# Two edits to a two-layer gated cross-attention kernel: layer-norm variance spread over all partitions, and slot-attention keys loaded from padded rows

## The reference, cut to what matters

```python
x = x + tanh(g_xattn[0]) * L0_xattn(layernorm(x), ctx, masks, ...)   # 16-head cross attention, ctx is (16, 1500, 128)
x = x + tanh(g_ffn[0])   * L0_ffn(layernorm(x), ...)                 # 16 experts, top 4, and a shared one
x = x + tanh(g_xattn[1]) * L1_xattn(layernorm(x), ctx, ...)          # slot attention, 3 rounds
x = x + tanh(g_ffn[1])   * L1_ffn(layernorm(x), ...)                 # 32 experts, top 2

def layernorm(x):            # over the 128 features, no weights
    return (x - mean(x)) / sqrt(var(x) + 1e-5)

# slot attention, three rounds, per batch: 56 slots, 1500 keys
scores = (rmsnorm(slots) @ Wq.T) @ (rmsnorm(P) @ Wk.T).T / sqrt(128)
attn   = softmax(scores, axis=slots);  attn = attn / (attn.sum(axis=keys) + 1e-6)
slots  = gru_cell(attn @ (rmsnorm(P) @ Wv.T), slots, ...)
```

## Time and profile before

| | us |
|---|---|
| three runs of the kernel before | 616.84 (median), 612.61, 617.85 |
| the profiled execution | 618.72 |
| its span | 616.9 |
| granted TensorE clock, mean over the span | 0.891 of full |

### The profile page before, as it was taken

The page is one execution under the profiler, slowest core; times in us unless marked ns, Lnnn a source line. Parts: engine busy times, 40 slices in busy tenths (PEclk is TensorE's granted clock), DMA queues, the critical chain, the costliest instruction groups (busy, mean ns, idle before and its releaser), DMA issues.

```text
span 616.9 us, 17523 instructions
## 1 busy us (share of the span) xinstructions
PE 491.4 (80%) x6216; PEld 375.7 (61%) x6216; DVE 385.0 (62%) x1149; ACT 323.5 (52%) x959; POOL 220.4 (36%) x414
## 2 busy tenths in 40 slices
PE   3687888887687899699999997889999856039990
PEld 2522224554474454289999996789899734039990
DVE  1569964555635544458989996779899845103332
ACT  3363664344322122378988986678988731023330
POOL 5366852122420000135445453435445400622241
PEclk9797987889986799989999998999999975559996
DMA  8887743343219999800000399910000099130003
GB/s 250 175 201 173 222 150 102 100 112 110 76 28 256 228 205 171 315 3 2 4 3 0 86 247 225 212 37 2 3 0 1 2 387 428 40 95 12 28 29 102
DMA packets 52589, 74.36 MB, mean 121 GB/s; under 512 B 6853, under 2 KB 46198, under 8 KB 51510
## 3 DMA queue, kind: packets, MB, share of 16 engines
q1 hardware_dynamic: 48380, 61.78, 40.9%
q0 software_dynamic: 1424, 7.81, 3.5%
q10 hardware_dynamic: 2730, 4.03, 2.2%
HBM read 69.07 MB, written 4.54 MB: 119 GB/s over the span
## 4 chain that ended last, share of the span: by engine, by line
PE 55%; DVE 13%; DMA 11%; SPq 7%; ACT 4%; issue 4%; POOL 3%; POOLq 1%; ACTq 0%; DVEq 0%
PE ps L1597 12%; PE ps L1611 8%; PE ps L1583 7%; SPq L562 6%; PE ps L1528 4%; PE ps L1727 4%; PE ps L1741 3%; DMA region<-in_wo 3%; DMA work<-in_kv_blk 3%; PE ps L1562 2%; POOL xe_scratch L746 2%; PE ps L1465 2%; DVE sumsq L991 2%; DMA region<-in_ctxT 2%; PE ps L1436 2%
## 5 line engine op out<-in xcount | busy, mean ns | idle before, releaser
L859 ACT ACTIVATE work<-ps,nb,rkey 125x56 f32<-125x56 f32 x576 | 173.3, 467 | 6.5 <-DVE nb L1200 6.3
L1597 PE MATMUL ps<-work,region 128*64 128x96 f32 (+1 forms) x2304 | 106.4, 249 | 4.0 <-issue 2.9
L1597 PEld LDWEIGHTS ps<-work,region 128*64 128x64 f32 (+1 forms) x2304 | 102.3, 138 | 8.2 <-issue 4.8
L1611 PE MATMUL ps<-region,work 125*64 125x129 f32 x1152 | 75.3, 278 | 5.1 <-issue 2.7
L704 POOL TENSOR_TENSOR work<-work,rs 125x336 f32<-125x336 f32 x96 | 71.9, 749 | 7.5
L1611 PEld LDWEIGHTS ps<-region,work 125*64 125x64 f32 x1152 | 65.5, 138 | 8.5 <-POOL work L704 3.7
L702 POOL TENSOR_TENSOR rs<-rs,rkey 125x6 f32<-125x6 f32 x96 | 19.3, 201 | 112.9 <-DVE rs L1212 112.8
L1197 DVE TENSOR_REDUCE ps<-ps 125x6 f32<-125x336 f32 x96 | 48.8, 508 | 6.6 <-PE ps L1597 6.3
L1208 DVE TENSOR_REDUCE sm<-work 125x6 f32<-125x336 f32 x96 | 47.4, 494 | 1.4 <-ACT work L859 1.3
L1583 PE MATMUL ps<-GI,work 112*64 112x112 f32 (+3 forms) x288 | 34.5, 314 | 6.9 <-DVE work L1221 2.5
L631 POOL TENSOR_TENSOR region<-early_w 125x768 f32<-125x768 f32 x16 | 29.1, 1820 | 22.4 <-DMA early_w<-in_ctx 22.0
(11 more groups left out here) (298 smaller groups left out, 970.4 us busy)
## 6 DMA issues: line engine op xcount, KB each, us to landing
region<-in_w SPq DMA_DIRECT2D x6, 2048.0 KB, 18.4
region<-in_ctxT SPq DMA_DIRECT2D x16, 750.0 KB
early_w<-in_ctx SPq DMA_DIRECT2D x16, 672.0 KB
region<-in_ctx SPq DMA_DIRECT2D x16, 672.0 KB
work<-in_ctxT_blk SPq DMA_DIRECT2D x22, 187.5 KB
early_w<-in_w POOLq DMA_DIRECT2D x1, 4096.0 KB, 13.7
region<-in_ctx_blk ACTq DMA_DIRECT2D x11, 187.5 KB
early_w<-in_ctx_blk ACTq DMA_DIRECT2D x10, 187.5 KB
```

Of the source, the lines that this page charges most:

```text
L859: i = act.activation(shares_of(p, a, h)[:, c, :], ps[:CP, 2 + 2 * a + h, c * S:(c + 1) * S], ACT.Exp, bias=nb[:, a, q:q + 1], scale=rkey[: ...
L1597: mm = pe.matmul(ps[r0:r1, 2 + 2 * a + h, c * S:c * S + WIDE], keysT[:, s, c0 + r0:c0 + r1], qT[:, p, a * S:a * S + WIDE], start=True, sto ...
L1611: mm = pe.matmul(ps[i * COL:(i + 1) * COL, bank, 0:KW], A[:CP, p % 2, i, h, c * S:c * S + COL], keys[:, 2 * p + i, h * CH + c, :], start=( ...
```

## The change

Two edits that do not touch one another.

**The norm.** PE now multiplies each half of `sq` with the whole matrix of 1/128, so that the variance comes out in all 128 partitions (banks 2 and 3). ACT takes the square root of 448 columns per half, DVE the reciprocal of 448 columns per half and then the product with `cen`. The diagonal matrices and the product with ones are gone, and so are their semaphores.

**The keys.** The host gives a second copy of the context in which each key has 129 columns, the last one zero. A partition's 12 keys are then one run of 6,192 bytes in both memories, where there were 12 runs of 512 bytes. The transfer now writes the 129th column too, so POOL waits for the batch's three transfers before it writes the root mean squares there, also in group 0, and two of the four calls for group 1 stand in later phases.

```diff
-                        sp.dma_start(keys[p0:p1, s, :, 0:128],
-                                     ctx_b[g * GB + s, p0:p1, :].rearrange("p (c d) -> p c d", c=CC)).then_inc(ld_keys[s], 16)
+                        sp.dma_start(keys[p0:p1, s, :, :].rearrange("p c d -> p (c d)"),
+                                     t["ctx_wide"][g * GB + s, p0:p1, :]).then_inc(ld_keys[s], 16)
...
                 for s in (2 * p, 2 * p + 1):
-                    if g:
-                        gp.wait_ge(u_mm, (g * UNITS - TWO + p + 1) * STEPS)
+                    gp.wait_ge(ld_keys[s], (g + 1) * 48)
                     gp.tensor_copy(keys[:, s, :, 128:KW], rms[:, g * GB + s, :].unsqueeze(2)).then_inc(key_col, 1)
...
-                if c == UNITS - 2 and g + 1 < GROUPS:
-                    key_rms(g + 1, 0)
-                    key_rms(g + 1, 1)
-                if c == UNITS - 1 and g + 1 < GROUPS:
-                    key_rms(g + 1, 2)
-                if c == 0 and g:
-                    key_rms(g, 3)
+                if c >= UNITS - 2 and g + 1 < GROUPS:
+                    key_rms(g + 1, c - (UNITS - 2))
+                if c < 2 and g:
+                    key_rms(g, c + 2)
...
-                act.wait_ge(ln_var, k + 1)
-                act.activation(ln_s[:, :], ps[:, 2, 0:NT], ACT.Sqrt, bias=eps_ln[:, :]).then_inc(ln_sd, 1)
+                for h in range(2):
+                    act.wait_ge(ln_var, 2 * k + h + 1)
+                    act.activation(rstd[:, half(h)], ps[:, 2 + h, 0:HALF], ACT.Sqrt, bias=eps_ln[:, :]).then_inc(ln_sd, 1)
...
-                v.wait_ge(ln_sd, k + 1)
-                v.reciprocal(ln_s[:, :], ln_s[:, :]).then_inc(ln_rec, 1)
-                v.wait_ge(ln_rec, k + 1)
-
-                diag = rstd.rearrange("p (n d) -> p n d", n=NT)
-                for j0, j1 in ((0, 4), (4, NT)):
-                    v.tensor_tensor(diag[:, j0:j1, :], ident[:, :].unsqueeze(1).to_broadcast([128, j1 - j0, 128]),
-                                    bcast(ln_s[:, j0:j1], 128), ALU.mult).then_inc(ln_diag, 1)
                 for h in range(2):
-                    v.wait_ge(ln_bc, 2 * k + h + 1)
-                    v.tensor_tensor(xln[:, half(h)], cen[:, half(h)], ps[:, h, 0:HALF], ALU.mult).then_inc(ln_out, 1)
+                    v.wait_ge(ln_sd, 2 * k + h + 1)
+                    v.reciprocal(rstd[:, half(h)], rstd[:, half(h)]).then_inc(ln_rec, 1)
+                    v.wait_ge(ln_rec, 2 * k + h + 1)
+                    v.tensor_tensor(xln[:, half(h)], cen[:, half(h)], rstd[:, half(h)], ALU.mult).then_inc(ln_out, 1)
...
-                for j in range(NT):
-                    pe.wait_ge(ln_sq, 2 * k + (1 if (j + 1) * 128 <= HALF else 2))
-                    mm = pe.matmul(ps[:, 2, j:j + 1], sq[:, j * 128:(j + 1) * 128], mean_w[:, 0:1], start=True, stop=True)
-                mm.then_inc(ln_var, 1)
                 for h in range(2):
-                    pe.wait_ge(ln_diag, 2 * k + h + 1)
-                    pe.wait_ge(ln_cent, 2 * k + 2)
-                    pe.matmul(ps[:, h, 0:HALF], ones[:, :], rstd[:, half(h)], start=True, stop=True).then_inc(ln_bc, 1)
+                    pe.wait_ge(ln_sq, 2 * k + h + 1)
+                    pe.matmul(ps[:, 2 + h, 0:HALF], mean_w[:, :], sq[:, half(h)], start=True, stop=True).then_inc(ln_var, 1)
...
+        "ctx_wide": np.pad(ctx.reshape(B, CP, CC, D), ((0, 0), (0, 0), (0, 0), (0, KW - D))).reshape(B, CP, CC * KW),
```

More of the change, by code:

```diff
@@ L96, in build_program @@
         cen, sq, rstd = (ln_tiles[:, k * T:(k + 1) * T] for k in range(3))
-        ln_s = sb("ln_s", [128, NT])
         folded = sb("folded", [128, 2 * H * 128])
@@ L306, in build_program @@
         ln_rec = sem("ln_rec")
-        ln_diag = sem("ln_diag")
-        ln_bc = sem("ln_bc")
         ln_out = sem("ln_out")
```

## The result

| | before | after |
|---|---|---|
| median of 4 runs, us | 614.73 (610.56 to 617.85) | 621.52 (620.37 to 624.12) |
| ratio of the runs | | 1.0118, 95% interval 1.0066 to 1.0170 |
| profiled execution, us | 618.72 | 621.35 |
| its span, us; granted clock | 616.9; 0.891 | 619.6; 0.894 |

What follows compares the result with a forecast made beforehand. PE was taken to bound most of the span, losing 12.0 us at slot attention's passage between groups to late keys and slow instructions. Norms +9.7 and keys -6.8 made +2.9 on the 616.84 median: 619.7 us, range 612.5 to 625.

Steps and rivals of the forecast that it cites:

- The norms as a whole: All four norms plus the half clock after the third: +9.7 us, bounds +8.7 and +11.
- The reciprocals: DVE in each norm: 2.95 us per 448 columns, two per norm; second norm +3.0 us, third +4.1.
- the first norm: First norm: DVE ends about 2.6 us later, hidden by waits for a mask and weights, so nothing.
- The fourth norm: Fourth norm: ends 7.8 us after its first square root starts, 513.8 against 512.1, so +1.7 us.
- The clock after the third norm: Start of slot attention: first matmuls and queries fall in the half clock, +0.9 us, between 0 and 2.
- The keys: Slot attention's passage from group 0 to group 1: gives back 6.8 us of 12.0 lost, bounds -12.0 and -3.
- The floor: Passage between the groups: four undisturbed phases would take 35.8 us against 47.75, so 12.0 us are lost.
- The price of a run: Group 1's key load: 0.35 us per 6.1 KB run, 44 us in all, engines full until 392.
- The residue: Passage between the groups: losses up to 392 stay while engines are full, 2.96 + 1.1 + 1.09 = 5.2 us.
- A: Passage: instruction gaps go with the late keys, all 12.0 us return, net -2.3, 614.5 us; chance 30%.
- B: Key load: long runs cost 0.41 us or more, slow instruction queue behind them, +7.5, 624.3 us; chance 15%.
- C: Key load: not sped up at all, only the norms show, +9.7, 626.5 us; chance 7%.

Runs made afterwards that it cites:

- e6_lnexp: Changed kernel with its eight DVE reciprocals replaced by a logarithm and exponential on ScalarE; 612.21 us, 0.9972 of the kernel before.
- e1_keys_only: Kernel before with only the three edits of the keys, norms as before; 611.91 us, 0.9949 of the kernel before.
- e3_no_load: Changed kernel without the load of group 1's keys, so group 1 computes with group 0's; 610.50 us, one execution.
- e9_one_slot: e6_lnexp with SP waiting for one slot's transfers to land before issuing the next slot's; 618.69 us, one execution.
- e4_traffic_passage: Changed kernel with group 1's key load replaced by equal traffic at the same time into places nobody reads; 613.23 us, one execution.
- e7_pairs: Kernel before with wide key rows, two slots per 12 KB run and half as many transfers; 611.68 us, 0.9966 of the kernel before.

## Why the prediction came out as it did

The time, 621.5, lies 1.8 us above the forecast and in its range. That is closer than the reasoning was: the median of the kernel before came out at 614.73 beside these runs and not at the 616.84 that I had added to, and this 2.1 us of luck hides part of the error. The change itself was forecast at +2.9 us and measured at +7.3. The ratio, +1.2%, is just past the 1% inside which I had put 75%. One term explains nearly all of it: what the keys give back was set too large by some 4 us. The norms as a whole, +9.7 forecast, cost +9.3 by the runs of the norm alone.

**The reciprocals: right.** 2.95 us, worked out from two shapes of the earlier trace rows, measured 2,950 ns; second norm +3.0 and third +4.1 as worked out. `e6_lnexp` shows that the norm's loss is in them. That the sums fit to a tenth is in part chance: the change's second and third norms take the same time in each profile that shows them (11.3 and 12.6), the old ones do not. Second, third and fourth together took 27.8 us in the profile before, 29.8 in its second one and 30.4 in `e1_keys_only`, against 37.7: +7.3 to +10.0. In the first norm I had costed them at nothing, 2.6 us without cover; after, the weights landed at 15.75 us and DVE stood on the chain, in the profile before they landed at 22.95 and it would not have. It depends on the execution; no run separates it.

**The fourth norm: +2.9 for +1.7.** I took the products of the mean from one execution, in which they took 2.23 us because the clock fell only within them. With the same norm they took 2.80 in the second profile (norm 11.37) and 3.35 in `e1_keys_only` (norm 11.92), at the half clock as after (3.36); against 11.92 the new norm costs 1.9, near the forecast. The chain behind the square root was right; the excess is the clock at the norm's start.

**The clock after the third norm: +0.9 forecast, not shown.** The first series took 1.95 us for 1.07, but it took 1.95 in the second profile of the unchanged kernel and in `e1_keys_only` too, 1.11 us behind DVE in both. So the full clock there belonged to one execution, and no run shows that the change costs this 0.9. Slot attention as a whole got shorter by 1.4 us with a passage shorter by 2.2.

**The keys: the step that failed**, -6.8 forecast, -2.2 at the passage and -3.1 (-5.2 to -1.1) by the runs of the keys alone. Three parts of it:
- The floor. I took four loop phases, 35.8 us; written-out ones with no traffic take 36.8 (`e3_no_load`). The loss before was 11.0, not 12.0.
- The price of a run. 0.35 us is right for one slot under way (`e9_one_slot`), but with the backlog that this kernel builds it is 0.39, close to my upper bound. The engines stay full to about 397 and not 392.
- The residue, the part that was furthest off: 5.2 us, the losses of one execution up to 392, two gaps and a slow update. After, 7.2 us of gaps and 1.1 of a slow update are left. The gaps come wherever PE runs into a block of instructions that is not there, at the pace at which blocks come through full engines, and their lengths differ between executions. The pace was misread as well: the 7.6 us each, from 5 packets in 38 us, count one more that came when the engines were emptying; while they were full, the packets stood 8 to 10 us apart.

**The rivals.** A, all gaps go: wrong, by the timeline after, and by `e4_traffic_passage`, where they come though no keys are waited for. B, slow long runs: half right; the price moved towards its 0.41, but no wait for `keysT` came. C, no faster load: the load did become shorter (787 engine-us for 951), yet the passage gained little, so its change, +9.7, lies nearer to the measured +7.3 than my +2.9 does, for another reason. What I had not listed is that a load may get 17% cheaper and give back a fifth of the loss. I read that as a loss per microsecond of full engines, while the bytes, 12.3 MB at some 250 GB/s, stay; the runs agree with it but do not single it out.

**The better version.** The keys alone, the pairs, and either with the logarithm and exponential come out at 0.995 to 0.997 of the kernel before and 0.983 to 0.986 of the changed one; the intervals of three of the four lie below 1, by a hair. The best by its median ratio is the keys alone, 0.9949.

## What to carry to other kernels

Before spreading a per-row statistic over all columns to save small steps, price the elementwise reciprocal for the wide shape from two shapes in the trace: here 7 columns cost 0.20 us and 448 cost 2.95, twice in each norm, on a chain with nothing beside it. When a profile shows "issue" gaps inside a series, look whether the engine is fetching new instructions and whether the DMA engines are full. Then moving the transfer under a loop that is past its first round takes them away (one execution each, with traffic that nobody reads), and longer runs and fewer descriptors hardly help; fewer bytes were not tried. Look also at the granted clock behind each gap, which adds to its cost. And take a second profile of the unchanged kernel before a stage's time goes into a sum. Two halves of a change should be run apart: one was worth -3 us and the other +9.

## What the runs showed of the hardware

- Instruction packets (16 KB) stand 8 to 10 us apart while the 16 DMA engines are full and PE runs code written out, with runs of 512 bytes and 6 KB alike, and 6.2 us apart in the mean when they are empty; PE is not stopped in the latter case. Every "issue" gap over 0.5 us in the passage of the kernels before and after ends 2.9 to 3.6 us behind the start of the microsecond of a packet.
- A gap of 2.5 to 3.4 us in a series can be followed by 2 to 3 us at the half clock (granted 0.50 in 390:393 after, in 377:379 before, in 378:381 in `e7_pairs`), which adds some 1.1 us.
- Full engines alone cost PE nothing: 10.00 of 10.00 us busy in 325:335 at 246 GB/s, in a loop whose body it had already run.
- Loads into 112 + 13 and 128 partitions ran at 229 to 268 GB/s with runs of 6 KB, and with runs of 12 KB (`e7_pairs`) at 327 in 350:357 and 241 to 274 after that; one run of 6.1 KB took 0.39 us with a backlog and 0.35 with one slot under way.
- DVE's reciprocal takes 202 ns for 7 columns of f32 and 2,950 for 448, 6.2 ns for each further column. ScalarE's logarithm and exponential of the same 448 took 0.63 and 0.57 us, with a table load of 1.28 us ahead of each.
